# Token rules and a layer of attention and experts: the transposed rows of a rule group, copied out of PSUM by one engine or by two

## The reference

```python
base_embeds = base_embeddings[token_ids]            # [8, 512, 64]
rule_indices = token_rules[token_ids]               # 0..99
rule_matrices = rule_transform[rule_indices]        # [8, 512, 64, 64]
h = jnp.einsum('bsd,bsde->bse', base_embeds, rule_matrices)
```

## Time and profile before

| what | value |
|---|---|
| median of three runs | 615.68 us |
| lowest and highest run | 615.65 and 620.51 us |
| the profiled execution's own time | 619.58 us |
| its span, first to last instruction | 617.5 us |
| mean granted TensorE clock | 0.923 |
| TensorE matmul busy | 499.3 us (81%) |
| VectorE busy | 410.7 us (67%) |
| ScalarE busy | 287.2 us (47%) |
| GpSimd busy | 228.3 us (37%) |

### The profile page before, as it was taken

One profiled execution on the slowest core, in us unless ns is written; L12 is line 12 of the kernel. 1 busy time (PEld: TensorE's weight loads), 2 busy tenths in 40 slices (PEclk: granted clock), 3 DMA queues, 4 the chain that ended last, 5 costly groups with the idle time before them and its releaser, 6 DMA issues.

```text
span 617.5 us, 9436 instructions
## 1 busy us (share of the span) xinstructions
PE 499.3 (81%) x2732; PEld 268.7 (44%) x2732; DVE 410.7 (67%) x1003; ACT 287.2 (47%) x581; POOL 228.3 (37%) x375
## 2 busy tenths in 40 slices
PE   0066603778679896999999999999999989999985
PEld 0035501234444342445544544454454444575753
DVE  5532486645215874978869877895975776665577
ACT  0203301025545543456564565556456546547664
POOL 5664356463225300340254145122413313181542
PEclk9998755559979997999999999999999999999989
DMA  8815212733381062440440422044042200000000
GB/s 234 312 59 152 79 36 61 179 95 103 95 229 40 14 155 53 102 113 5 100 114 2 102 63 60 1 104 113 1 96 68 53 2 2 11 2 10 11 2 17
DMA packets 21791, 47.05 MB, mean 76 GB/s; under 512 B 6248, under 2 KB 11576, under 8 KB 21680
## 3 DMA queue, kind: packets, MB, share of 16 engines
q1 hardware_dynamic: 15408, 32.23, 21.5%
q0 software_dynamic: 4752, 8.20, 4.9%
q10 hardware_dynamic: 1584, 6.03, 3.0%
HBM read 9.97 MB, written 11.01 MB: 34 GB/s over the span
## 4 chain that ended last, share of the span: by engine, by line
PE 54%; DVE 19%; issue 8%; DMA 6%; POOL 6%; ACT 3%; SPq 3%; another core or an unknown queue 0%; DVEq 0%; ACTq 0%; POOLq 0%
PE bank L1274 14%; PE bank L1260 10%; PE bank L1240 7%; PE bank L1202 4%; PE bank L1224 4%; DVE mx L997 3%; POOL emb_sorted L527 2%; DMA ctxT<-in_table,ids 2%; PE bank L1196 2%; PE bank L1197 2%; DVE r_sb L1055 2%; POOL ctxT L517 2%; PE bank L1132 2%; POOL r_sb L591 2%; DMA ks<-qk_l 1%
## 5 line engine op out<-in xcount | busy, mean ns | idle before, releaser
L997 DVE TENSOR_REDUCE mx<-bank 128x1 f32<-128x512 f32 x256 | 170.5, 687 | 83.5 <-PE bank L1260 75.3
L591 POOL TENSOR_TENSOR r_sb<-r_sb 128x256 f32<-128x256 f32 x174 | 91.0, 523 | 251.8 <-DVE r_sb L1073 171.4
L671 ACT ACTIVATE prob<-bank 128x512 f32<-128x512 f32 x256 | 139.0, 597 | 58.5 <-PE bank L1240 43.0
L1260 PE MATMUL bank<-ks,qs 96*128 96x512 f32 x256 | 122.7, 487 | 14.4 <-DVE mx L997 9.7
L1274 PE MATMUL bank<-prob,xa 128*64 128x512 f32 x448 | 123.5, 630 | 0.7 <-ACT ctxT L685 0.7
L1260 PEld LDWEIGHTS bank<-ks,qs 96*128 96x128 f32 x256 | 50.9, 199 | 130.8 <-issue 109.5
L1240 PE MATMUL bank<-qs,ks 97*128 97x512 f32 x224 | 78.1, 430 | 0.0
L738 ACT ACTIVATE r_sb<-bank,stay 128x512 f32<-128x512 f32 x56 | 37.1, 687 | 44.9 <-PE bank L1197 44.6
L1240 PEld LDWEIGHTS bank<-qs,ks 97*128 97x128 f32 x224 | 38.4, 194 | 15.6 <-issue 11.1
L527 POOL DMA_INDIRECT emb_sorted<-ctxT,pos x32 | 32.0, 1001 | 22.6 <-DMA emb_sorted<-ctxT,pos 11.7
L517 POOL DMA_INDIRECT ctxT<-in_table,ids x32 | 32.4, 1011 | 21.3 <-DMA ctxT<-in_table,ids 8.6
(11 more groups left out here) (167 smaller groups left out, 659.3 us busy)
## 6 DMA issues: line engine op xcount, KB each, us to landing
qs<-qk_h SPq DMA_DIRECT2D x64, 128.0 KB
ks<-qk_h SPq DMA_DIRECT2D x56, 128.0 KB
qs<-qk_l SPq DMA_DIRECT2D x32, 128.0 KB
ks<-qk_l SPq DMA_DIRECT2D x28, 128.0 KB
emb_sorted<-front ACTq DMA_DIRECT2D x4, 608.0 KB
y_sorted<-y_out POOLq DMA_DIRECT2D x19, 128.0 KB, 2.7
e_in<-emb_sorted POOLq DMA_DIRECT2D x9, 256.0 KB, 3.2
emb_sorted<-front ACTq DMA_DIRECT2D x3, 640.0 KB
```

The source lines that it names most:

```text
L591: nc.gpsimd.tensor_tensor(a[:, at:at + width], src[:, 0:width], src[:, width:2 * width], ALU.add).then_inc(S["pool_chain"], 1)
L671: nc.scalar.activation(prob[:, step % NPROB, u % 2, :], bank[u % NST][:], ACT.Exp, scale=SC).then_inc(S["exp_done"], 1)
L997: V.tensor_reduce(mx[:, u // 16, u % 16:u % 16 + 1], bank[3 + n % 2][:], AX.X, ALU.max).then_inc(S["mx_done"], 1)
L1260: M(bank[3 + n % 2][:], qs[0:96, nb % 2, h, tt * 128:(tt + 1) * 128], ks[0:96, nb % 2, h, :], start=True, stop=True).then_inc(S["s_ps"], 1)
```

## The change

ScalarE copies only the even half of a group's transposed rows (partitions 0 to 63 of the bank), and VectorE copies the odd half (partitions 64 to 127), in both parts. The odd half has a semaphore of its own, `eT_odd`. TensorE waits for both semaphores before `apply`, and before it writes the bank again. In the first loop VectorE now does, in the turn of g, the odd half of group g and then the `y_out` copy of group g - 1; the pieces of `look` stay behind the same `y_out` copies as before. In the second part the odd copy is among VectorE's extra tasks, which stand at the end of its step. Number, size and destination of the copies, and all DMAs, are as before.

```diff
@@ names of semaphores
-            scattered_0 scattered_1 eT_ps eT_ok y_ps y_ok xn_ready xa_ready w_h ones_ok w_ok xT_ps x_hi xs_ready
+            scattered_0 scattered_1 eT_ps eT_ok eT_odd y_ps y_ok xn_ready xa_ready w_h ones_ok w_ok xT_ps x_hi xs_ready
@@ drained()
             if kind == "rT":
                 eng.wait_ge(S["eT_ok"], b + 1)
+                eng.wait_ge(S["eT_odd"], b + 1)
@@ ScalarE, first part
-                for r in range(2):
-                    ins = nc.scalar.copy(eT[0:D, g % 2, r * 256:(r + 1) * 256], bank[g % 2][64 * r:64 * r + 64, 0:256])
-                ins.then_inc(S["eT_ok"], 1)
+                nc.scalar.copy(eT[0:D, g % 2, 0:256], bank[g % 2][0:64, 0:256]).then_inc(S["eT_ok"], 1)
@@ ScalarE, second part
-                            for r in range(2):
-                                ins = nc.scalar.copy(eT[0:D, ab % 2, r * 256:(r + 1) * 256], ring(a)[64 * r:64 * r + 64, 0:256])
-                            ins.then_inc(S["eT_ok"], 1)
+                            nc.scalar.copy(eT[0:D, ab % 2, 0:256], ring(a)[0:64, 0:256]).then_inc(S["eT_ok"], 1)
@@ VectorE, first part
             later = chain(look(1, 2), look(1, 3))
-            for g in range(NG[0]):
-                dve.wait_ge(S["y_ps"], g + 1)
-                store_sent(dve, g - 4)
-                V.tensor_copy(y_out[:, g % 4, :], bank[2 + g % 2][:, 0:4 * D]).then_inc(S["y_ok"], 1)
-                if 5 <= g < 9 or g >= 11:
-                    next(later, None)
+            def odd_rows(g, from_):
+
+                dve.wait_ge(S["eT_ps"], g + 1)
+                if g >= 2:
+                    dve.wait_ge(S["y_ps"], g - 1)
+                V.tensor_copy(eT[0:D, g % 2, 256:512], from_[64:128, 0:256]).then_inc(S["eT_odd"], 1)
+
+            for g in range(NG[0] + 1):
+                if g < NG[0]:
+                    odd_rows(g, bank[g % 2])
+                if g >= 1:
+                    dve.wait_ge(S["y_ps"], g)
+                    store_sent(dve, g - 5)
+                    V.tensor_copy(y_out[:, (g - 1) % 4, :], bank[2 + (g - 1) % 2][:, 0:4 * D]).then_inc(S["y_ok"], 1)
+                    if 6 <= g < 10 or g >= 12:
+                        next(later, None)
             run(later)
@@ VectorE, second part, extra tasks of a step
+                        if kind == "rT":
+                            odd_rows(ab, ring(a))
@@ TensorE, apply()
                 pe.wait_ge(S["eT_ok"], g + 1)
+                pe.wait_ge(S["eT_odd"], g + 1)
@@ TensorE, first part
                     if g >= 2:
                         pe.wait_ge(S["eT_ok"], g - 1)
+                        pe.wait_ge(S["eT_odd"], g - 1)
                     turn(g, bank[g % 2])
```

## The result

| | before | changed |
|---|---|---|
| median of 10 runs each, measured side by side | 619.65 us | 623.64 us |
| lowest and highest | 615.65 and 626.43 us | 621.67 and 626.46 us |
| ratio, 95% interval | | 1.0072 [1.0041, 1.0103] |
| the profiled execution | 619.58 us, clock 0.923 | 624.28 us, clock 0.907 |
| its span | 617.5 us | 622.5 us |

The changed kernel is 0.72% slower, which is 4.5 us of 619.65, by the interval 2.5 to 6.4 us. That is within 1%, on the slower side. The size forecast, + 3.05 us, lies in the interval. The absolute time does not lie in the range: the three runs of before shown ahead (median 615.68) have their median at the low end of that kernel's spread.

The account below looks back on a forecast made before the run. TensorE was taken to bound the kernel, through its waits for copies. First part + 2.3, steps (0, 0) and (0, 1) + 2.25, later gains - 1.5: + 3.05 us on 615.68, giving 618.7 us; range 614.2 to 622.6.

Parts of the forecast that it names:

- the last of the sum: Whole kernel: the effect of + 3.05 us added to the runs' median of 615.68 us, giving 618.7 us.
- First part, + 2.3: First loop: group 10's odd copy waits behind VectorE's gather, delaying TensorE's `apply(10)`, second `count` and `turn(12)`; + 2.3 us.
- passes one for one to the start of the second part: Between the parts: a delay of the last `y_out` copies moves the second part's start equally.
- Step (0, 0), + 1.85: Second part's first step: odd copies behind layernorm and row maxima delay the second `turn`; scores of (0, 1) + 1.85 us later.
- Step (0, 1), + 0.4: Second part's second step: odd copies behind the layernorm's rest and row maxima bring the lateness from + 1.85 to + 2.25 us.
- Step (0, 2), - 0.66: Second part's third step: two of TensorE's waits for copies shrink by 0.33 us each, - 0.66 us.
- rival B: New gaps keep TensorE at 1.2 GHz through (0, 0) to (0, 2): + 4 us on top, 622.7 us; chance 0.15.
- PV near 1.9 us in this step: Sign of rival B: PV taking near 1.9 us at (0, 1) or (0, 2).
- waits of 0.59 and 0.83 us: Argument against rival B: such waits between groups in (0, 1) had not brought the clock down before.
- Steps (0, 3) to (0, 5), - 0.83: Later second part: shorter copy waits win nothing in (0, 3), - 0.5 us in (0, 4), - 0.33 us in (0, 5).
- rival A: Both parts: odd copies are in time, so all six waits and the last gaps shrink; - 2.8 us, 612.9 us; chance 0.12.
- the 1.1 that the forecast named and left out: VectorE: some seven odd copies and their followers lose 0.08 us overlap each by the partition rule; 1.1 us, not summed.

Follow-up runs that it names:

- e1: The change in the first part only, ScalarE making both copies in the second part, against the kernel before: median 621.67 us, ratio 1.0033.
- e9: The changed kernel measured again, unaltered, against the kernel before: median 620.25 us, ratio 1.0030.
- e11: The changed kernel with odd copies of groups 10 to 12 moved ahead of the gather's wait, second part plain: median 620.38 us, 0.9984 of before.
- e4: The change in the first part only, with odd copies of groups 10 to 12 ahead of the gather's wait: median 619.44 us, 0.9996 of before.
- e2: The change in the second part only, against the kernel before: median 619.31 us, ratio 1.0016.
- e7: The kernel before with only the layernorm's pieces in (0, 0) and (0, 1) moved behind the row maxima: median 619.95 us, ratio 0.9999.
- e6: The kernel before, ScalarE making both copies, but each raising its own semaphore and TensorE waiting for both: median 620.70 us, ratio 1.0012.
- e3: The change in the second part only, with odd copies ahead of the layernorm's pieces in (0, 0) and (0, 1): median 615.89 us, 0.9942 of before.
- e5: The change in both parts, odd copies moved ahead of the gather's wait and of the layernorm's pieces: median 616.65 us, 0.9945 of before.
- e10: As e5, plus eight extra matmuls with unread results keeping TensorE busy ahead of (0, 0): median 614.22 us, 0.9936 of before.
- e8: The changed kernel with `apply` repeated ahead of the late `turn` in (0, 0) and (0, 1) to fill TensorE's gaps: median 620.49 us, 1.0013 of before.

## Why the prediction was right or wrong

**The base was wrong, and with it the absolute time.** The step that failed is the last of the sum: "for the median: 615.68 + 3.05 = 618.7 us". It took the median of three runs for the kernel's time, and gave the range only the uncertainty of the effect. The hundred runs of before beside the experiments have medians of 619.3 to 620.6 us. The profiled execution that I had, 619.58, was nearer to the middle than the median of three. The sum against that execution, 622.6, is 1.0 us below the first median of the changed kernel and 2.4 above the second. Put on 619.65, the forecast's own range of + 0.9 to + 5.2 is 620.6 to 624.9, and holds the measured 623.64.

**The size.** + 3.05 us was forecast. Measured are + 4.5 (2.5 to 6.4) and + 1.9 (- 0.5 to 4.1), at equal clock + 3.0 and + 2.6. The sum came out right in part by luck, as its terms show.

**First part, + 2.3.** Right: A grew by 2.1 us in the changed kernel, and is long in all four kernels with the plain loop (10.07 to 10.54 against 7.81 to 8.69), and in none of the four with the copies ahead (8.17 to 8.64). In time e1 shows + 1.6 at equal clock. That a delay "passes one for one to the start of the second part" can't be read from single profiles: GpSimd's way from its first gather of results to the loads, 48.08 us in before, was 46.99 in e9 and 50.17 in e1, a scatter as large as the effect. The times support it: 1.9 us between e9 and e11 at equal clock, 2.0 between e1 and e4.

**Step (0, 0), + 1.85.** Mis-sized: the step took 8.06 us (changed), 8.13 (e2), 8.21 (e11) and 8.29 (e9) against 7.89, so + 0.2 to + 0.4. But the length of this step goes with its part at 1.2 GHz: with ScalarE's copies it is 5.75 us where that part is 0 (e1) and 7.89 where it is 5.4 (before), and the four kernels here have 3.9 to 4.6. Against e7, with ScalarE's copies and 4.4 us (7.76), e2, e11 and e9 are + 0.4 to + 0.5. The second `turn` stands 0.94 us still in it, not the 2 us of the forecast. The term took for granted that the gathered rows come 3.46 us behind the step's scores, the difference between 138.77 in the earlier trace rows and 135.31 below. They came 1.67 us behind them (139.09 less 137.42). Before's timeline, GpSimd's last gather for sequence 1, and TensorE's scores of (0, 0):

```profile
134.76 0.95 POOL L535 DMA_INDIRECT hbuf<-y_sorted,pos  x1 [0.30 <-issue]
...
135.31 1.22 PE L1240 MATMUL bank<-qs,ks 97*128 97x512 f32 x2
```

The same two in e6, with its layernorm:

```profile
135.22 0.95 POOL L536 DMA_INDIRECT hbuf<-y_sorted,pos  x1 [0.30 <-issue]
...
137.59 0.42 DVE L897 TENSOR_REDUCE ln_s<-hbuf 128x4 f32<-128x256 f32 x1 [2.20 <-DMA hbuf<-y_sorted,pos]
...
135.90 1.22 PE L1243 MATMUL bank<-qs,ks 97*128 97x512 f32 x2
```

By G the rows came 4.01 us behind GpSimd's last gather in before, and 2.36 us in the changed kernel. My estimate: had they taken 4.01 there too, and passed on one for one, the step would have been 1.65 us longer, which with 0.2 is the 1.85 of the forecast. Is this an effect of the change? In the kernels whose second part is as before G is 3.83 and 4.21 (e1, e4), in the changed ones 2.36 to 2.50, but also 2.37 in e6, in which only a semaphore is new. Where the layernorm starts too late to tell G, the record of the DMA tells its landing: 2.5 us in e3, 2.7 in e5, 3.2 in e10 and, here, 3.5 in e7.

```profile
L535 POOL DMA_INDIRECT hbuf<-y_sorted,pos x1: 947/947/947, 134.0 to 134.0; - x1
...
DMA to landing us min/median/max: 3.5/3.5/3.5
```

So the landing lies anywhere between 2.3 and 4.2 us, with one profile of each kernel (two of the changed one), and the runs don't tie it to an edit. It may be chance. Its cause was not tried and stays open; the loads behind the gathers share their queue.

**Step (0, 1), + 0.4.** It took 7.57 us (changed), 7.23 (e2), 7.27 (e11), 7.17 (e9) against 6.65 to 6.88 in the five kernels with ScalarE's copies: + 0.5 to + 0.6 over before, and + 0.9 in the changed kernel, of whose step 1.5 us stood at 1.2 GHz. The mechanism was right and its price a little low.

**Step (0, 2), - 0.66.** Right at an undisturbed clock, and covered by the clock here. In e5, where the step has no part at 1.2 GHz, it took 10.50 us against 11.28, 11.28 and 11.25 in before, e1 and e4: - 0.78. In the kernels with the late copies it took 14.08 (changed), 12.59 (e2), 12.60 (e9) and 12.60 us (e11). In all four the clock had fallen ahead of it, behind the gap of 1.35 us in (0, 1). So here a part of **rival B** was right. The forecast's own sign for it was PV near 1.9 us in this step: it took 1.98 in the changed kernel, 1.56 to 1.65 in the other three, 1.08 in e8. But rival B's size was not there: of the step 5.8 us stood at 1.2 GHz in e2, e9 and e11, no more than the 5.1 and 6.4 us in e7 and e6, which have before's copies and took 12.18 and 12.51 us. Only the first profile of the changed kernel had more (10.7 us). The forecast had held against the rival that waits of 0.59 and 0.83 us had not brought the clock down. The Trainium skill, page "TensorE: Matmul & The Clock Gate", section "Part 1: The HAM clock gate (the "warmup" mystery)", says that idle stretches throttle the array back to half rate; this case agrees in kind, with 1.22 us for two scores behind the gap and 0.72 where e8 has filled it.

Taken together, (0, 0) to (0, 2) are + 2.1 to + 2.3 us over before in e2, e9 and e11 (+ 3.9 in the first profile of the changed kernel), against + 1.6 in the forecast. The nearness is luck: (0, 0) was put too high by over 1 us, and the early fall of the clock is not in the sum.

**Steps (0, 3) to (0, 5), - 0.83.** C as a whole can't tell it: it is 26.34 to 27.19 us in the four kernels with the plain second part, and 24.75 (e1) to 26.92 in those with ScalarE's copies. In step (0, 5) alone, wholly at 2.4 GHz in all profiles, e2, e3, e5, e8 to e11 have 5.83 to 5.92 us, and before, e1, e4, e6, e7 have 5.97 to 6.36. That is 0.2 us of the 0.33 forecast there, though the changed kernel's own profile has 6.12.

**The gain where nothing holds it back.** e5 is 0.55% faster than before, 3.4 us, near the - 2.8 of rival A. Nothing shows that it is rival A's gain: at equal clock there are 0.8 us, in the three steps with a like clock 0.9, and the rest is a higher mean clock whose cause is open. Rival A itself fell, as the odd copies were late at both places.

**The overlap on VectorE.** Of two `y_out` copies in the earlier trace rows the second starts 0.34 us behind the first. Around an odd copy the starts are 0.45 and 0.46 us apart (68.41, 68.86, 69.32 in the changed kernel), while the small operation behind the odd copy of 144.80 starts 0.35 us after it. The Trainium skill, page "VectorE: DVE Perf Modes", section "Two Vector instructions with no wait between them", says that an instruction is held when an input starts in another quarter of the partitions than the first input of the last instruction that read the same memory, or its output in another than the last output there. The trace agrees in both cases: a `y_out` copy reads PSUM from partition 0 behind a read of PSUM from 64, the small operation reads SBUF. My own wording in the forecast was too wide, as it left out that the memories are counted apart. The price is 0.11 us per boundary; of the two boundaries at 68 to 70 us that is at most 0.2 us, and no run shows the 1.1 that the forecast named and left out.

## What to carry to other kernels

Giving half of a small job to a second engine that is idle enough on average costs time if in that engine's order the job stands behind an instruction that waits for a DMA; read, for each moved instruction, what is right ahead of it and what that waits for, and move it ahead of the waiting one if its input is there. Here that turned + 0.3 to + 0.7% into - 0.5%, with not one instruction less; at equal clock + 2.6 to + 3.0 us into - 0.8. The price of the order, some 3.5 us, is shown; of the gain over before most goes with the clock, and only some 0.9 us could be read as the copies' own. And a kernel's base time should come from as many runs as its spread asks for: the median of three lay 4 us from the middle, as much as the whole effect. Last, before two profiles of one step are compared, look at how much of the step each had at the low clock.

## What the runs showed of the hardware that was not expected

- The time of this kernel on one core follows TensorE's granted clock from one execution to the next. 94 of before's 100 runs lie from 614.85 us at a clock of 0.925 to 624.26 us at 0.905, the other six above. The profiles show how: the same step of the same kernel is granted 1.2 GHz for a longer part in one execution than in another. Of (0, 2), 10.7 us stood at 1.2 GHz in the changed kernel's first profile and 5.8 in its second (e9), and the step took 14.08 and 12.60 us. The two scores of (0, 0) took 1.22 us in before and 0.73 in e1, whose second part is the same.
- The last of GpSimd's gathers for sequence 1, the same instruction in all kernels, landed 2.3 us (e6) to 4.2 us (e4) behind its start, with values of 2.5, 2.7, 3.2, 3.5 and 3.8 us in between. No run shows what sets it.
- A gap of 1.35 us in TensorE's work went with the clock at 1.2 GHz at the next step's start in four profiles of four. With the gap at 0.40 us (e8), and in the eight kernels that never had it, that step started at 2.4 GHz.
- Eight matmuls whose results nobody reads raised the mean clock from 0.920 to 0.930, and moved the time by at most a few tenths of a per cent beyond e5.
